# Mask products of the attention scores in 64x64 tiles of the matrix array in place of 64x128

## The chip, the cores and the metric

The kernel runs on one core of one Trainium2 chip. The metric is the device time of one execution in microseconds. Three executions of the kernel before took 1553.94, 1553.43 and 1547.58 us, with a median of 1553.43.

## The reference

Two layers run one after the other on 4096 tokens of 128 values (16 batches of 256 tokens). Each layer normalises the tokens, computes an attention `s` and a mixture of experts `g` from them, and adds `s * silu(g)` to the tokens. Cut to what matters here:

```python
# layer 0: differential attention, 16 heads of 8, two attention maps per head, causal
att1 = softmax(where(causal, q1 @ k1.T * scale, -inf))
att2 = softmax(where(causal, q2 @ k2.T * scale, -inf))
y = (att1 - lam * att2) @ v          # then normalised per head, and @ c_w
# layer 1: 16 heads of 8, each query sees a window of the last 128 keys
scores = q @ k_window.T / sqrt(8)    # keys before the start count as score 0
ctx = softmax(scores) @ v_window     # then @ wo.T + bo
```

In the first layer a query must not see later keys; in the second it must see neither later keys nor keys that lie 128 or more positions back. In both, -1e30 is added to a score that must not count, and that addition is what the change is about.

## The kernel before, in words

`build` (L1455) runs, for each layer, a layer norm, a router, the experts and the attention (`build_attention`, L709). The attention is laid out over five engines that run the same schedule (`schedule`, L873): a step for each batch, with a prologue, a loop of turns of four steps, and an epilogue. A step has `UNITS` slots (12 in the first layer, which has A = 2 attention maps, 6 in the second). In each slot TensorE makes two **groups** of score products, i = 0 and i = 1, one for each half of the heads (`both_scores`, L1118).

A group serves two streams at once. `scores_for_max` (L1071) makes scores with queries on the partitions, from which DVE takes row maxima (L1370). It runs ahead by `AHEAD` slots, so it works on the next batches. `scores` (L1093) makes scores with keys on the partitions, of the current batch, with the negated maxima folded in, and ACT takes their exponentials (L1259). The first stream reads the stack on partitions of half `i` and writes `s_bank[i]`; the second reads half `1 - i` and writes `t_bank[i]`. Each stream has two banks of 512 fp32 columns, so group i of a slot may begin when DVE and ACT have read what group i of the slot before wrote (`lone_wait` on `s_free` and `t_free`, L1126 and L1131).

For each j from 0 to 5 a product of the one stream and a product of the other are issued in turn, by `score_matmul` (L1057). j = 0 and j = 1 are the **mask products** (L1062): an identity times a table of mask values. A block of scores has 128 partitions and 128 or 256 columns. Only the two 64x64 blocks on its diagonal, or in windowed cases two more, have a mask that is neither all zero nor constant; whole blocks are masked by extra rows of the stack. The mask table (`R.mask_diag_q` and others, L1490 to L1493) has 64 rows, the same in both halves of the partitions, and the identity `R.eye` (L1489) is a 64x128 table in two forms: for j = 0 the identity stands in the left 64 columns and zeros in the right, for j = 1 the other way. So product j adds the mask to the 64 partitions of its block, and writes zeros to the other 64. The columns that it writes are those of block j (`one_block`, L1065: 64 columns of each of the 2 or 4 heads of the bank; `two_blocks`, L1068: 128 of each of 2 heads). The first has `start=True` and the second doesn't. The remaining 2 or 4 products (L1063) add a head's scores each, 256 or 128 columns, with `start=False`.

What widths meet in a slot follows from the code. In the second layer all mask products have 256 columns. In the first layer `scores_for_max` has 256 where n + 4 modulo 6 is 0 or 1 and 128 otherwise, and `scores` has 256 where n modulo 3 is 2 and 128 otherwise. Slots 0, 1, 4, 6, 7 and 10 have 128 columns in both streams; slots 2 and 8 with 256 in both; slots 3, 5, 9 and 11 with one of each.

Between groups TensorE does fp32 work. After both groups of a slot `weigh` (L1138) multiplies the exponentials with the values in 32-column tiles (L1153, then L1156, four strips that share a bank), and `general_use` (L1196) does one or two of: projections (L1044, L1051, L1188), transposes (L1164, L1172, L1179). DVE also splits the projected queries and keys into three bf16 pieces (`split`, the last part is L1358, in slot 2 of the first layer and slot 5 of the second). When they are ready, SP copies them with twelve DMAs into the stack (`fill_stack`, L999 to L1007). TensorE waits for these copies before the first maxima of that batch (`stacked`, L1125), in slot 8 of the first layer and slot 3 of the second.

Of the kernel before, what the change touches and what calls it, by code (L numbers as in the profile page):

```python
# [39 lines left out]
HALF = 64  # L40
# [665 lines left out]
def build_attention(nc, R, D, layer):  # L706
# [76 lines left out]
    with ExitStack() as ctx:  # L783
# [251 lines left out]
        def _(pe):  # L1035
# [21 lines left out]
            def score_matmul(j, bank, half, per, rows, fine, mask, left, right):  # L1057

                tile = slice(half * HALF, half * HALF + (HALF if j < 2 else rows))
                bank = bank.rearrange("p (m w) -> p m w", m=per)  # L1060
                if j < 2:
                    return nc.tensor.matmul(fine(bank, j), R.eye[tile, j, :], mask[tile], start=(j == 0), stop=True, skip_group_check=(j > 0))  # L1062
                return nc.tensor.matmul(bank[:, j - 2, :], left(j - 2)[tile], right(j - 2)[tile], start=False, stop=True, skip_group_check=True)  # L1063

            def one_block(at):  # L1065
# [481 lines left out]
```

## Time and profile before

| | |
|---|---|
| median of 3 executions | 1553.43 us |
| the profiled execution | 1545.69 us |
| its span, first to last instruction | 1544.0 us |
| TensorE matmul busy | 1163.1 us, 75% |
| DVE busy | 841.1 us, 54% |
| ACT busy | 782.4 us, 51% |
| GpSimd busy | 626.6 us, 41% |
| mean granted TensorE clock | 0.88 |
| mask products (L1062), matmuls | 2304, 235.8 us |
| score products (L1063), matmuls | 3072, 273.3 us |

The profiled execution is one of its own beside the three. Its rows name an engine, a line and a tile shape: 64*128 is a weight tile of 64 rows (contraction) and 128 columns (output partitions), and 64x256 beside it is the moving operand, 256 columns. Matmuls are pipelined and the end of one is modelled, so the busy time of TensorE is an upper bound, and the starts are what a reader should go by. PEld is TensorE's weight load. "x4" in a timeline is a merged run of four instructions; where two groups overlap, the start is that of the first of each. The first layer's attention runs from about 300 us to 860 us of the span, the second's from about 1150 us on.

### The profile page before, as it was taken

What the parts mean: (1) busy time and instruction counts of PE and PEld (TensorE: products, weight loads), DVE (VectorE), ACT (ScalarE), POOL (GpSimd) and SP (SyncE); (2) the same over time, 40 slices, a digit from 0 to 9 for tenths busy, and PEclk for the clock granted to TensorE, in tenths of its full rate; (3) what the DMA queues carried; (4) which work ended last, traced back from release to release, by engine and by line L of the source; (5) the groups of instructions that cost most, each with busy time, mean ns of one, the idle gap of its engine ahead of it and who ended that gap; (6) DMA issues with size and microseconds to landing.
All of it is one profiled execution on the core that took longest, in us unless ns stands there. A gap on an engine that the chain in (4) does not pass through costs nothing. (4 is left out here: it accounts for less than half of the span.)

```text
span 1544.0 us, 38917 instructions
## 1 busy us (share of the span) xinstructions
PE 1163.1 (75%) x12538; PEld 870.9 (56%) x12538; DVE 841.1 (54%) x1694; ACT 782.4 (51%) x1828; POOL 626.6 (41%) x968
## 2 busy tenths in 40 slices
PE   1458888768888788888888156888866788888885
PEld 1357888634555555555554146788853555555553
DVE  5184555456766676677641338455534655556551
ACT  2163544415777677777765130344441655555553
POOL 3254445200355445545554315444521234334434
PEclk9999999968999999999997555799985988878887
DMA  5401222231232223222300240122222112221210
GB/s 146 112 0 39 59 56 55 38 86 47 63 80 58 52 51 85 64 51 60 82 18 8 69 110 0 43 54 56 57 42 61 50 49 55 60 56 49 61 42 24
DMA packets 144971, 86.71 MB, mean 56 GB/s; under 512 B 16610, under 2 KB 138356, under 8 KB 144820
## 3 DMA queue, kind: packets, MB, share of 16 engines
q1 hardware_dynamic: 136116, 66.85, 16.6%
q0 software_dynamic: 8704, 17.84, 4.9%
q8 instruction: 95, 1.56, 0.4%
q14 instruction: 56, 0.46, 0.1%
HBM read 30.19 MB, written 15.73 MB: 30 GB/s over the span
## 5 line engine op out<-in xcount | busy, mean ns | idle before, releaser
L1370 DVE TENSOR_REDUCE at_maxima<-ps 128x2 f32<-128x512 f32 (+1 forms) x576 | 375.1, 685 | 270.8 <-PE ps L1063 250.0
L1259 ACT ACTIVATE at_probs<-ps 128x512 f32<-128x512 f32 x576 | 324.0, 597 | 133.2 <-PE ps L1063 115.8
L1062 PE MATMUL ps<-tables 64*128 64x256 bf16 (+1 forms) x2304 | 235.8, 266 | 154.0 <-DMA stack<-at_pieces 58.3
L1063 PE MATMUL ps<-stack 62*128 62x256 bf16 (+3 forms) x3072 | 273.3, 260 | 4.5 <-issue 4.5
L664 ACT ACTIVATE ex_hid<-ps,ex_w 128x128 f32<-128x128 f32 x576 | 163.8, 370 | 178.1 <-PE ps L639 130.8
L1062 PEld LDWEIGHTS ps<-tables 64*128 64x128 bf16 x2304 | 94.5, 97 | 263.9 <-issue 230.7
L598 POOL DMA_INDIRECT ex_rows<-xn_rows,ex_ids_now x144 | 149.8, 1041 | 93.8 <-PE ps L631 42.7
L1063 PEld LDWEIGHTS ps<-stack 62*128 62x128 bf16 (+1 forms) x3072 | 170.7, 101 | 16.3 <-issue 4.1
L639 PE MATMUL ps<-ex_rowsT,ex_w 128*128 128x128 f32 x1152 | 161.4, 284 | 24.1 <-DVE ex_rowsT L688 23.3
L695 DVE COPY ex_w<-weights 128x1156 f32 x144 | 114.0, 791 | 104.8 <-issue 103.8
L649 PE MATMUL ps<-ex_w,ex_hid 128*128 128x128 f32 x1152 | 154.8, 278 | 15.6 <-ACT ex_hid L664 7.2
L639 PEld LDWEIGHTS ps<-ex_rowsT,ex_w 128*128 128x128 f32 x1152 | 143.2, 195 | 33.2 <-issue 30.1
L649 PEld LDWEIGHTS ps<-ex_w,ex_hid 128*128 128x128 f32 x1152 | 141.8, 194 | 17.8 <-issue 17.7
L949 POOL DMA_INDIRECT at_chosen_y<-list_out,at_slot x128 | 126.6, 989 | 57.5 <-issue 33.1
L1153 PE MATMUL ps<-at_probs,at_v 128*32 128x256 f32 x1536 | 135.5, 427 | 3.3 <-ACT at_probs L1259 3.3
L970 POOL TENSOR_TENSOR at_s_rows<-at_s_rows,at_silu 128x256 f32<-128x256 f32 x32 | 23.3, 729 | 226.3 <-ACT at_s_rows L1311 226.3
L1156 PE MATMUL ps<-at_probs,at_v 128*32 128x128 f32 x1536 | 86.0, 295 | 1.6 <-issue 1.6
L1156 PEld LDWEIGHTS ps<-at_probs,at_v 128*32 128x32 f32 x1536 | 54.9, 120 | 42.9 <-issue 15.2
L424 PE MATMUL ps<-rt_at_tile,rt_at_place 128*128 128x72 f32 x256 | 55.2, 422 | 29.0 <-POOL rt_at_place L391 29.0
L1264 ACT COPY at_weighed_t<-ps 128x512 f32<-128x512 f32 x96 | 56.7, 591 | 39.2 <-remote 25.1
L894 POOL COPY at_xb<-xnT 128x256 f32<-128x256 f32 (+1 forms) x32 | 13.5, 421 | 155.1 <-PE ps L1054 96.6
L424 PEld LDWEIGHTS ps<-rt_at_tile,rt_at_place 128*128 128x128 f32 x256 | 54.8, 333 | 30.4 <-POOL rt_at_place L391 30.4
(181 smaller groups left out, 1610.4 us busy)
## 6 DMA issues: line engine op xcount, KB each, us to landing
stack<-at_pieces SPq DMA_DIRECT2D x192, 128.0 KB
stack<-at_pieces SPq DMA_DIRECT2D x192, 64.0 KB
list_out<-ex_result SPq DMA_DIRECT2D x144, 64.0 KB
weights<-in_L_w SPq DMA_DIRECT2D x4, 1024.0 KB, 6.1
weights<-in_L_w SPq DMA_DIRECT2D x16, 256.0 KB, 6.6
xn_rows<-xn SPq DMA_DIRECT2D x8, 512.0 KB, 3.2
ex_rows<-xn_rows,ex_ids_now POOLq DMA_INDIRECT x144, 2.5
x<-in_L_attn_x SPq DMA_DIRECT2D x4, 512.0 KB, 6.0
```

The costliest lines, as they stand in the source:

```text
L598: nc.gpsimd.indirect_dma_start(rows[q][:], None, D["xn_rows"], bass.IndirectOffsetOnAxis(ids[:, q:q + 1], 0)).then_inc(loaded[q], 16)
L639: last = nc.tensor.matmul(hid_ps[q % 2][:, hb * P:(hb + 1) * P], w[q][:, W1 + hb * P:W1 + (hb + 1) * P], rowsT[q % 2][:], start=True, stop ...
L649: last = nc.tensor.matmul(out_ps[q % 2][:, 0:C], hid[q % 2][:, hb, :], w[q][:, W2 + hb * C:W2 + (hb + 1) * C], start=(hb == 0), stop=(hb = ...
L664: last = nc.scalar.activation(hid[q % 2][:, hb, :], hid_ps[q % 2][:, hb * P:(hb + 1) * P], gelu, bias=w[q][:, B1 + hb:B1 + hb + 1])
L695: nc.vector.tensor_copy(w[q][:], weights[:, bass.ds(e, 1), :].rearrange("p o w -> p (o w)"))
L949: nc.gpsimd.indirect_dma_start(chosen_y[t][k][:], None, D["list_out"], bass.IndirectOffsetOnAxis(slot[:, i:i + 1], 0)).then_inc(gathered, 16)
L1062: return nc.tensor.matmul(fine(bank, j), R.eye[tile, j, :], mask[tile], start=(j == 0), stop=True, skip_group_check=(j > 0))
L1063: return nc.tensor.matmul(bank[:, j - 2, :], left(j - 2)[tile], right(j - 2)[tile], start=False, stop=True, skip_group_check=True)
L1153: nc.tensor.matmul(strip, v[p][:, 0, h, :], pr[:, part, at:at + SEQ], start=True, stop=False)
L1156: last = nc.tensor.matmul(strip[:, P:SEQ], v[p][:, 1, h, :], pr[:, 2, at:at + P], start=False, stop=True)
L1259: nc.scalar.activation(probs[:, (n // 3) % 2, n % 3, i * 512:(i + 1) * 512], t_bank[i], ACT.Exp, scale=SCALE).then_inc(t_free, 1)
L1370: nc.vector.tensor_reduce(by_half[:, h0:h0 + heads, a], s_bank[i].rearrange("p (m k) -> p m k", k=P * (late + 1)), AX.X, ALU.max).then_inc ...
```

## The change

Each mask product writes only the 64 partitions of its own block. The weight is the 64x64 identity, and the output begins at partition 0 for j = 0 and at partition 64 for j = 1. Both products have `start=True`. The score products are as they were; their first write to a region that no mask product wrote now fills it.

```diff
                 if j < 2:
-                    return nc.tensor.matmul(fine(bank, j), R.eye[tile, j, :], mask[tile], start=(j == 0), stop=True, skip_group_check=(j > 0))
+                    out = slice(j * HALF, (j + 1) * HALF)
+                    return nc.tensor.matmul(fine(bank[out], j), R.eye[tile, 0, 0:HALF], mask[tile], start=True, stop=True)
                 return nc.tensor.matmul(bank[:, j - 2, :], left(j - 2)[tile], right(j - 2)[tile], start=False, stop=True, skip_group_check=True)
```

## Rows read from the trace of the kernel before

**Rows 1.** Windows over the steady part of both attention stages: from:to, length, busy times

```profile
core 0: us, PE busy (x) PEld busy (x) DVE busy (x) ACT busy (x) POOL busy (x), PEclk, DMA share, GB/s
353.00:784.00 431.00, 363.23 (x5440) 235.38 (x5436) 297.82 (x485) 305.20 (x627) 198.87 (x337) 0.97 0.25 62
1190.00:1491.00 301.00, 249.50 (x2852) 162.97 (x2849) 170.88 (x342) 170.89 (x392) 112.99 (x185) 0.85 0.22 56
```

**Rows 2.** Waits: who waited for whom, us in total, times, longest

```profile
DVE at_maxima L1370 <- PE ps L1063: 250.0, 216, 11.1
PEld ps L1062 <- issue: 230.7, 396, 4.3
ACT at_probs L1259 <- PE ps L1063: 115.8, 181, 6.9
...
PE ps L1062 <- DMA stack<-at_pieces: 58.3, 26, 12.1
```

**Rows 3.** Groups by line and shape: count, busy us, mean ns, idle before

```profile
L1062 PE MATMUL ps<-tables 64*128 64x256 bf16 x1280 | 171.5, 298 | 120.2 <-DMA stack<-at_pieces 58.3 <-DVE at_maxima L1370 33.7 <-issue 15.2
...
L1062 PEld LDWEIGHTS ps<-tables 64*128 64x128 bf16 x2304 | 94.5, 97 | 263.9 <-issue 230.7 <-DMA stack<-at_pieces 23.0
```

**Rows 4.** Timeline of TensorE, first layer, 600 to 607 us: start, length, what

```profile
600.27 0.29 PE L1062 MATMUL ps<-tables 64*128 64x128 bf16 x4 [0.68 <-ACT at_probs L1259]
600.38 0.40 PE L1063 MATMUL ps<-stack 62*128 62x256 bf16 x4
600.77 0.29 PE L1062 MATMUL ps<-tables 64*128 64x128 bf16 x4
...
603.60 0.64 PE L1153 MATMUL ps<-at_probs,at_v 128*32 128x256 f32 x8
604.05 0.40 PE L1156 MATMUL ps<-at_probs,at_v 128*32 128x128 f32 x8
604.39 1.16 PE L1188 MATMUL ps<-wo,at_yT 128*128 128x128 f32 x8
605.48 0.39 PE L1062 MATMUL ps<-tables 64*128 64x256 bf16 x4
605.71 0.39 PE L1063 MATMUL ps<-stack 62*128 62x128 bf16 x8
605.93 0.38 PE L1062 MATMUL ps<-tables 64*128 64x256 bf16 x4
606.15 0.39 PE L1063 MATMUL ps<-stack 62*128 62x128 bf16 x8
606.47 0.66 PE L1164 MATMUL ps<-ident,at_weighed_t 128*128 128x128 f32 x4
607.12 0.38 PE L1062 MATMUL ps<-tables 64*128 64x256 bf16 x4
607.25 0.47 PE L1063 MATMUL ps<-stack 64*128 64x256 bf16 x6
```

**Rows 5.** Timeline of TensorE, second layer, 1293 to 1297 us

```profile
1292.96 0.61 PE L1062 MATMUL ps<-tables 64*128 64x256 bf16 x4
1293.36 0.64 PE L1063 MATMUL ps<-stack 62*128 62x256 bf16 x4
1293.79 0.64 PE L1062 MATMUL ps<-tables 64*128 64x256 bf16 x4
1294.22 0.64 PE L1063 MATMUL ps<-stack 64*128 64x256 bf16 x4
1294.78 1.08 PE L1153 MATMUL ps<-at_probs,at_v 128*32 128x256 f32 x8
...
1296.84 0.61 PE L1062 MATMUL ps<-tables 64*128 64x256 bf16 x4
```

**Rows 6.** Window over the same stretch; PEclk is the number after the POOL column

```profile
1290.00:1298.00 8.00, 8.00 (x55) 4.79 (x56) 3.79 (x7) 4.71 (x11) 0.40 (x1) 0.50 0.19 50
```

**Rows 7.** Timeline of SP's queue and of TensorE around one batch's stack copies

```profile
639.24 8.73 SPq L1007 DMA_DIRECT2D stack<-at_pieces  x12
...
651.11 0.39 PE L1062 MATMUL ps<-tables 64*128 64x256 bf16 x4 [1.44 <-DMA stack<-at_pieces]
```

## The prediction

> **What bounds the kernel now.** I read the windows first. In the two attention stages TensorE is busy for 84% and 83% of the time, DVE and ACT for 57 to 71%, at a mean granted clock of 0.97 and 0.85 [rows 1]. The list of waits says who is late: DVE idles 250.0 us and ACT 115.8 us for score products, TensorE idles 58.3 us in 26 places for the stack transfers [rows 2]. So TensorE leads, in a loop through DVE and ACT, and at one place a batch the transfers lead. 1280 of the 2304 mask products have 256 columns [rows 3], the other 1024 have 128.
>
> The timeline shows what they cost. The two row halves run at once, so four products are two pairs. From the first mask product of a group to its first score product it is 0.11 us with 128 columns (600.27 to 600.38), 0.23 with 256 (605.48 to 605.71), 0.13 where the halves differ (607.12 to 607.25) [rows 4]. That is streaming: a pair of 128 columns takes 0.055, since four score pairs last 0.22 (605.71 to 605.93). Nothing is lost between masks and scores; both use 64x128 tiles.
>
> **What a change of tile costs.** After the four pairs that start at 606.15 the 128x128 transposes start at 606.47: 0.32, of which 0.22 is streaming, so 0.10 is lost. A change of columns alone costs as much: L1156 (128x32) runs two rounds of four at 604.05, half as wide as L1153's, which last 0.45 together (603.60 to 604.05, the same tile and no gap); 0.34 later L1188 (128x128) starts, 0.11 more than the 0.23 that they stream [rows 4]. At a granted clock of 0.50, the level of 1.2 GHz, two score pairs that stream in 0.43 (1293.36 to 1293.79) are followed by L1153 after 0.56 (1294.22 to 1294.78): 0.13 lost [rows 5, 6]. The Trainium skill, TensorEngine Tiling (Array Packing), section Tiling Modes, says that a change of the tiling mode, not of the tile alone, drains TensorE. By that rule, and the trace agrees, this change pays a drain that the kernel now does without.
>
> **The change, part by part.**
> 1. It removes half of the mask streaming: the four products go to four tiles. L1153's four strips, four column tiles that write one bank, run together (eight products of 256 columns in 0.45), so I take the four as one round: 0.055 for 128 columns, 0.11 for 256, 0.20 at half clock.
> 2. It adds a switch from masks to scores in every group. No row has 64x64 to 64x128. Bounds: 0, if only the row split counted, and 0.13, the largest seen; I take 0.10, since the column-only row is nearest. Masks to scores is then 0.155 in place of 0.11 (+0.045), 0.21 in place of 0.23 (I count -0.01, for the four starts), 0.21 in place of 0.13 (+0.08), and at half clock 0.33 in place of 0.40 (-0.07).
> 3. It adds a switch from scores to the next masks where these follow directly. Between the two groups of a unit there often is a pause: 600.38 to 600.77 is 0.39 with 0.22 of streaming. A pause over 0.10 hides the drain and the first group's delay too; with that cover gone 0.10 more would show. There is none at 605.71 to 605.93 [rows 4]. The weight loads of masks sat idle for "issue" 396 times [rows 2] in 576 groups, which leaves 31% without: I take one unit in three in the first layer. In the second layer all products are 256 wide, the queue runs ahead (1293.36 to 1293.79 is streaming alone [rows 5]), and I take three in four; one in three and all are the bounds. Ahead of a unit's first group stands fp32 work, whose switch is paid already.
> 4. Weight loads of 64 columns replace loads of 128. A load's record has 97 ns [rows 3] and lies beside the product before it. Bounds: 0, hidden as now, and 0.05 a group, half of that record exposed; I take 0, since L1153's loads, in column tiles as well, cost nothing visible at 603.60 beyond the switch.
> 5. No wait, DMA, or instruction of DVE, ACT, SP or POOL is added, moved or removed.
>
> **What lies on the path.** A batch's stack copies start when L1358 is done: twelve issues from 639.24 on take 8.73 us, and TensorE takes its next mask at 651.11 after 1.44 idle [rows 7]. From slot 2 to slot 8 of the first layer that transfer sets the time, and there five units at about 0.09 each (0.44) vanish in the 1.44. In the second layer the copies start after the split in slot 5 and are needed in slot 3; a wait is 58.3 / 26 = 2.2 us on average [rows 2], again more than three units add. So 7 of 12 units count in the first layer (112 in 16 batches) and 3 of 6 in the second (48).
>
> First layer: the seven slots (8 to 11, 0 to 2) hold three groups of 128, two of 256, two mixed: (3 x 0.045 - 2 x 0.01 + 2 x 0.08) / 7 = +0.04 a group. A unit costs 0.04, and in one of three 0.14 more (the other group and the drain): 0.087 x 112 = 9.7 us. Second layer: at full clock -0.01 + 3/4 x (0.10 - 0.01) = +0.06, at half clock -0.07 + 3/4 x (0.13 - 0.07) = -0.025; a clock of 0.85 is 30% at half, so +0.034 x 48 = 1.7 us. Together 11.4. Not all is passed on, since a group also waits for DVE or ACT (0.68 at 600.27 [rows 4]) that were late with other work; I take 0.7, below TensorE's share of 0.84: **+8 us**. The profiled execution took 1545.69 us, 1.7 over its span of 1544.0; it becomes 1553.7. The median of the three runs, 1553.43, is 7.7 above that execution, and I carry the sum over to it: 1561.4.
>
> **Rivals.**
> - Faster: a column split inside one row split needs no drain. Place: masks to scores. A group then gains 0.055 (128), 0.115 (256), about 0.08 (mixed), 0.20 at half clock. First layer 4/3 x 0.08 x 112 = 12.0, second 1.75 x (0.7 x 0.115 + 0.3 x 0.20) x 48 = 11.8, times 0.7: -17, so 1537. It decides once a switch costs less than about 0.05. For it: no row shows exactly this pair of tiles. Against: the 0.11 of L1156 to L1188. Chance 0.15. (The page's section Overview, in the Trainium skill, promises up to twice the rate where the stationary operand has at most 64 columns, as here.)
> - Nothing to measure: pauses and the loop through DVE and ACT take up the 11 us as well. For it: most groups pause for longer than a switch. Against: DVE's 250.0 us of waiting. 1553, chance 0.20.
> - The four products don't overlap, so the change doesn't do what it says: the switches come on top of the old streaming. (0.10 + 1/3 x 0.20) x 112 = 18.7, second layer about 0.27 x 48 = 13, times 0.7: +22, 1575. L1153's strips speak against it. Chance 0.05.
> - The slower weight load of part 4: (0.067 x 112 + 0.0875 x 48) x 0.7 = 8 us more, 1569. For it: nothing covers a load right after a drain. Chance 0.05. The Trainium skill, TensorEngine Tiling (Array Packing), section Restrictions and Gotchas, says that column tiling excludes Fast Weight Load; its page TensorE: Matmul & The Clock Gate, section LDWEIGHTS, gives columns / 1.2 ns, an estimate of 53 ns for 64.
> - The clock: less is streamed, and the second layer runs at half clock for 60% in place of 30%. A unit at half clock lasts 1296.84 - 1292.96 = 3.88 [rows 5], at full clock about half of that: 0.3 x 48 x 1.94 x 0.7 = 20 on top, 1581. For it: the clock in that stage is unsteady (0.85). Against: TensorE's pauses don't grow. Chance 0.05.
>
> **How the numbers follow.** My own case has 0.50 and spans 1556 to 1573: from a third of the sum to its full (0.087 x 192 + 0.034 x 96) = 20 us, if no unit is covered. Half a per cent, about what a measurement of this kernel can tell from no change, is 7.8 us: 1545.7 to 1561.2. Rather more than half of my case lies above (0.30), which with the last three rivals makes 0.45 slower; 0.20 of it and the second rival make 0.40 the same; 0.15 faster. The range 1543 to 1577 leaves out most of the first rival and the last one.
>
> **What the profile of after would show.** Right: L1062 as 64x64, the four mask products of a group starting within 0.02; masks to scores about 0.16 with 128 columns and 0.21 with 256; scores to masks 0.10 over streaming where they follow directly; transfer waits somewhat shorter in total than 58.3. Wrong: masks to scores of 0.06 and 0.11 (the first rival), of 0.21 and 0.32 (no overlap), or a clock well under 0.85 in the second attention stage.

## The result, and the profile after

The kernel after takes 1588.35 us (median of 4, 1585.47 to 1591.51), the kernel before in the same comparison 1550.51 (median of 4). The ratio is 1.0245, with an interval of 1.0207 to 1.0284: 38 us slower, where +8 was forecast. The profiled execution took 1585.47 us and its span is 1583.5, against 1544.0. Every line from L1062 on has moved down by one, so L1063 are now the mask products and L1064 the score products.

The page of after: the row of TensorE, and its groups (busy us, mean ns, idle before).

```profile
PE 1235.1 (78%) x12538; PEld 836.1 (53%) x12538; DVE 842.8 (53%) x1694; ACT 793.2 (50%) x1828; POOL 630.0 (40%) x968
...
L1063 PE MATMUL ps<-tables 64*64 64x256 bf16 (+1 forms) x2304 | 194.5, 289 | 125.9 <-DMA stack<-at_pieces 52.6
L1064 PE MATMUL ps<-stack 64*128 64x128 bf16 (+3 forms) x3072 | 280.0, 269 | 0.0
...
L1063 PEld LDWEIGHTS ps<-tables 64*64 64x64 bf16 x2304 | 79.7, 107 | 269.6 <-issue 231.3
```

The change does what it says: the tile is 64*64, and the busy time of the mask products falls from 235.8 to 194.5 us. The transfer wait is somewhat shorter, 52.6 in place of 58.3 [rows 2], as forecast. A weight load's record grows from 97 to 107 ns [rows 3].

The list of waits of after, to be held against [rows 2]:

```profile
DVE at_maxima L1371 <- PE ps L1064: 271.0, 227, 11.1
...
PEld ps L1063 <- issue: 231.3, 484, 3.8
ACT at_probs L1260 <- PE ps L1064: 130.6, 213, 5.6
...
PE ps L1063 <- DMA stack<-at_pieces: 52.6, 20, 12.1
```

DVE and ACT wait longer for TensorE, by 21 and 15 us. The idle time of a mask's weight load keeps its sum, but it comes 484 times in place of 396, in 626 groups (526 with four mask products, 100 with two): many groups that followed the scores directly now stand behind a short gap.

The timeline of TensorE of after, first layer, answers to [rows 4]:

```profile
619.01 0.30 PE L1063 MATMUL ps<-tables 64*64 64x256 bf16 x4
619.24 0.40 PE L1064 MATMUL ps<-stack 62*128 62x128 bf16 x8
619.57 0.66 PE L1165 MATMUL ps<-ident,at_weighed_t 128*128 128x128 f32 x4
620.15 0.30 PE L1063 MATMUL ps<-tables 64*64 64x256 bf16 x4
620.39 0.39 PE L1064 MATMUL ps<-stack 62*128 62x128 bf16 x6
620.71 0.30 PE L1063 MATMUL ps<-tables 64*64 64x256 bf16 x4
...
622.91 0.25 PE L1063 MATMUL ps<-tables 64*64 64x128 bf16 x4 [0.20 <-issue]
623.09 0.39 PE L1064 MATMUL ps<-stack 62*128 62x256 bf16 x4
```

From the first mask product to the first score product it is 0.18 with 128 columns (622.91 to 623.09; it was 0.11), 0.23 with 256 (619.01 to 619.24, as before), and 0.24 where the halves differ (620.15 to 620.39; it was 0.13). Scores to masks, 620.39 to 620.71, takes 0.32, of which some 0.22 is streaming: 0.10 lost, where [rows 4] lose nothing.

Windows show where the 38 us lie. They are read from the two profiled executions, whose spans differ by 39.5 us. Each kernel is cut at its first mask product of a layer and at the first exponentials (L1260) of batch 0, of batch 15, and the last. The rows are, in order: layer 0 up to the first exponentials, its steady part, its last batch, the same three of layer 1, and the end. The number behind the POOL column is the mean granted clock. First before, then after:

```profile
319.40:353.40 34.00, 27.04 (x174) 15.71 (x174) 23.98 (x38) 3.39 (x8) 4.35 (x6) 0.60 0.22 56
353.40:812.10 458.70, 386.73 (x5789) 250.52 (x5790) 312.30 (x511) 325.68 (x670) 212.99 (x362) 0.97 0.24 59
812.10:839.60 27.50, 25.86 (x263) 14.59 (x261) 2.12 (x6) 18.28 (x39) 14.05 (x25) 0.71 0.04 11
1163.40:1190.10 26.70, 20.09 (x114) 11.95 (x116) 15.89 (x30) 2.80 (x8) 0.53 (x2) 0.56 0.14 36
1190.10:1506.40 316.30, 264.51 (x3018) 172.60 (x3015) 178.21 (x358) 181.69 (x418) 119.35 (x197) 0.85 0.21 54
1506.40:1520.20 13.80, 12.33 (x134) 7.31 (x132) 1.48 (x5) 9.18 (x21) 6.75 (x13) 0.88 0.09 25
1520.20:1544.00 23.80, 9.69 (x60) 5.78 (x60) 2.29 (x6) 4.39 (x12) 8.20 (x13) 0.66 0.08 22
```

```profile
320.70:357.70 37.00, 34.84 (x178) 15.30 (x178) 25.12 (x38) 3.36 (x7) 4.35 (x6) 0.50 0.20 51
357.70:833.10 475.40, 423.31 (x5788) 235.34 (x5784) 312.50 (x510) 331.27 (x671) 213.96 (x362) 0.93 0.23 57
833.10:865.40 32.30, 31.54 (x264) 15.86 (x264) 3.11 (x6) 19.37 (x38) 14.04 (x25) 0.66 0.04 9
1191.20:1219.00 27.80, 23.11 (x114) 9.94 (x114) 16.47 (x30) 2.83 (x9) 0.53 (x2) 0.50 0.13 34
1219.00:1537.60 318.60, 273.29 (x3037) 150.10 (x3034) 177.71 (x358) 185.15 (x418) 122.94 (x198) 0.85 0.21 55
1537.60:1558.50 20.90, 18.86 (x114) 8.87 (x114) 1.45 (x5) 9.75 (x21) 7.79 (x13) 0.50 0.07 20
1558.50:1583.50 25.00, 11.99 (x60) 7.42 (x60) 1.90 (x6) 4.37 (x12) 5.41 (x10) 0.50 0.04 10
```

Three findings. The steady part of layer 0 grows by 16.7 us, and its clock falls from 0.97 to 0.93. The steady part of layer 1 grows by 2.3, at an unchanged 0.85. And the five short stretches around them, which the prediction never looked at, grow by 3.0, 4.8, 1.1, 7.1 and 1.2: 17.2 us together, in 126 us. The first four (16.0 us) are the **one-stream steps**: a group serves one stream only (maxima ahead of batch 0, scores of batch 15) and has two mask products in place of four. In four of the five TensorE is now at 0.50, the level of 1.2 GHz, from end to end. The last batch of layer 1 goes from 13.8 us at 0.88 to 20.9 at 0.50.

### The profile page after: what moved, and what is told of

Same layout as the page of the kernel before. It is cut to its first block and busy times, and to the rows that moved or that the text cites. A ratio compares the mean times of both kernels' runs of the same rounds, so it can differ in the third digit from the quotient of the medians.

```text
span 1583.5 us, 38917 instructions
## 1 busy us (share of the span) xinstructions
PE 1235.1 (78%) x12538; PEld 836.1 (53%) x12538; DVE 842.8 (53%) x1694; ACT 793.2 (50%) x1828; POOL 630.0 (40%) x968
## 5 line engine op out<-in xcount | busy, mean ns | idle before, releaser
L1260 ACT ACTIVATE at_probs<-ps 128x512 f32<-128x512 f32 x576 | 330.0, 598 | 142.6 <-PE ps L1064 130.6
L1063 PE MATMUL ps<-tables 64*64 64x256 bf16 (+1 forms) x2304 | 194.5, 289 | 125.9 <-DMA stack<-at_pieces 52.6
L1064 PE MATMUL ps<-stack 64*128 64x128 bf16 (+3 forms) x3072 | 280.0, 269 | 0.0
L1063 PEld LDWEIGHTS ps<-tables 64*64 64x64 bf16 x2304 | 79.7, 107 | 269.6 <-issue 231.3
L598 POOL DMA_INDIRECT ex_rows<-xn_rows,ex_ids_now x144 | 148.8, 1034 | 96.5 <-PE ps L631 50.1
L1064 PEld LDWEIGHTS ps<-stack 64*128 64x128 bf16 (+1 forms) x3072 | 116.0, 98 | 77.1 <-issue 24.0
L949 POOL DMA_INDIRECT at_chosen_y<-list_out,at_slot x128 | 127.4, 995 | 57.1 <-issue 32.7
L1154 PE MATMUL ps<-at_probs,at_v 128*32 128x256 f32 x1536 | 141.1, 444 | 3.4 <-ACT at_probs L1260 3.4
L1265 ACT COPY at_weighed_t<-ps 128x512 f32<-128x512 f32 x96 | 56.7, 591 | 38.2 <-PE ps L1157 25.5
L1044 PE MATMUL ps<-xnT,wqk 128*128 128x256 f32 (+1 forms) x192 | 65.0, 456 | 9.8 <-POOL at_v L978 9.2
```

The costliest lines, as they stand in the source:

```text
L598: nc.gpsimd.indirect_dma_start(rows[q][:], None, D["xn_rows"], bass.IndirectOffsetOnAxis(ids[:, q:q + 1], 0)).then_inc(loaded[q], 16)
L949: nc.gpsimd.indirect_dma_start(chosen_y[t][k][:], None, D["list_out"], bass.IndirectOffsetOnAxis(slot[:, i:i + 1], 0)).then_inc(gathered, 16)
L1063: return nc.tensor.matmul(fine(bank[out], j), R.eye[tile, 0, 0:HALF], mask[tile], start=True, stop=True)
L1154: nc.tensor.matmul(strip, v[p][:, 0, h, :], pr[:, part, at:at + SEQ], start=True, stop=False)
L1260: nc.scalar.activation(probs[:, (n // 3) % 2, n % 3, i * 512:(i + 1) * 512], t_bank[i], ACT.Exp, scale=SCALE).then_inc(t_free, 1)
```

## The experiments

Eighteen kernels. The table gives, for each, the ratio to the kernel before with its interval, and length / mean granted clock of the windows cut as above: layer 0's first step (A), steady part (B), last batch (C); layer 1's first step (D), steady part (E), last batch (F).

Each row of windows comes from one profiled execution, and that is not always a middling one. Those of `e_edge` (1591.90 us, median 1584.56), `e_doubled_edge` (1601.69, median 1592.82) and `e_not89` (1587.92, median 1581.64) were the slowest of their four, that of `e_steady` (1565.05, median 1570.59) the fastest. E shows how far one trace can be trusted. In the seven kernels with before's order, products and waits in all of it (before, `e_layer0`, `e_only89`, `e_doubled_89` and the shifts) it lies between 316.0 and 320.0. With the change in layer 1's steady part it was 318.6 in after and 317.1 in `e_steady`, but 326.0 in `e_layer1` and in `e_not89`.

| kernel | ratio | A | B | C | D | E | F |
|---|---|---|---|---|---|---|---|
| before | 1 | 34.0 / .60 | 458.7 / .97 | 27.5 / .71 | 26.7 / .56 | 316.3 / .85 | 13.8 / .88 |
| after | 1.0245 [1.0207, 1.0284] | 37.0 / .50 | 475.4 / .93 | 32.3 / .66 | 27.8 / .50 | 318.6 / .85 | 20.9 / .50 |
| e_layer0 | 1.0164 [1.0125, 1.0204] | 37.0 / .50 | 478.0 / .92 | 32.3 / .66 | 26.7 / .50 | 317.9 / .85 | 13.0 / 1.00 |
| e_layer1 | 1.0070 [1.0042, 1.0099] | 34.1 / .60 | 458.3 / .97 | 25.0 / .91 | 27.8 / .50 | 326.0 / .85 | 21.0 / .50 |
| e_half | 0.9827 [0.9793, 0.9860] | 32.7 / .60 | 450.1 / .93 | 25.9 / .72 | 25.4 / .50 | 312.3 / .83 | 13.8 / .88 |
| e_doubled | 1.0710 [1.0665, 1.0756] | 40.4 / .50 | 516.5 / .92 | 29.7 / .86 | 29.8 / .50 | 345.3 / .85 | 24.0 / .50 |
| e_all64 | 1.0376 [1.0310, 1.0441] | 34.8 / .60 | 503.0 / .88 | 25.8 / .73 | 25.7 / .50 | 325.0 / .82 | 17.5 / .80 |
| e_grouped64 | 1.0282 [1.0212, 1.0353] | 38.8 / .59 | 487.2 / .92 | 27.6 / .72 | 27.1 / .50 | 319.3 / .84 | 12.0 / 1.00 |
| e_grouped128 | 1.0221 [1.0150, 1.0291] | 38.4 / .59 | 481.3 / .95 | 26.6 / .84 | 27.7 / .50 | 322.1 / .85 | 12.0 / 1.00 |
| e_fill_before | 1.0332 [1.0297, 1.0367] | 34.6 / .60 | 463.1 / .96 | 24.9 / .91 | 25.1 / .64 | 371.9 / .85 | 20.1 / .66 |
| e_fill_after | 1.0586 [1.0553, 1.0619] | 37.9 / .55 | 477.8 / .95 | 32.4 / .66 | 26.9 / .63 | 387.0 / .82 | 19.5 / .57 |
| e_steady | 1.0161 [1.0111, 1.0210] | 33.5 / .60 | 478.8 / .92 | 27.3 / .71 | 26.7 / .50 | 317.1 / .85 | 13.8 / .88 |
| e_edge | 1.0197 [1.0146, 1.0248] | 36.9 / .50 | 472.4 / .94 | 38.5 / .50 | 27.9 / .50 | 324.2 / .85 | 21.0 / .50 |
| e_doubled_edge | 1.0245 [1.0205, 1.0286] | 40.2 / .50 | 466.3 / .95 | 42.3 / .50 | 29.6 / .50 | 328.0 / .84 | 22.9 / .50 |
| e_not89 | 1.0205 [1.0151, 1.0260] | 36.6 / .50 | 472.7 / .95 | 31.9 / .66 | 27.8 / .50 | 326.0 / .83 | 19.6 / .57 |
| e_only89 | 1.0068 [1.0031, 1.0105] | 33.5 / .60 | 470.8 / .91 | 24.8 / .91 | 26.7 / .50 | 318.1 / .85 | 12.9 / 1.00 |
| e_doubled_89 | 1.0214 [1.0175, 1.0252] | 35.0 / .60 | 494.9 / .92 | 28.0 / .72 | 26.8 / .50 | 317.4 / .87 | 13.7 / 1.00 |
| e_shift2 | 1.0004 [0.9978, 1.0030] | 34.6 / .60 | 459.7 / .96 | 26.7 / .73 | 26.8 / .50 | 320.0 / .85 | 12.8 / 1.00 |
| e_shift4 | 0.9985 [0.9955, 1.0015] | 34.5 / .60 | 456.7 / .97 | 24.7 / .91 | 26.8 / .50 | 316.0 / .87 | 12.8 / 1.00 |
| e_shift7 | 1.0014 [0.9981, 1.0047] | 35.6 / .64 | 459.2 / .96 | 27.7 / .71 | 27.3 / .50 | 317.6 / .84 | 12.8 / 1.00 |

### The change in one layer

```diff
+                if j < 2 and layer == 0:
+                    out = slice(j * HALF, (j + 1) * HALF)
+                    return nc.tensor.matmul(fine(bank[out], j), R.eye[tile, 0, 0:HALF], mask[tile], start=True, stop=True)
                 if j < 2:
...
```

`e_layer1` has `layer == 1` there.

> The change in the first layer's attention alone. Two theories. S (switches): the two drains in each group of score products are paid on the path, and the lower clock is a by-product. C (clock): the change streams less, the granted clock falls more often, and that costs most of the 38 us. Both read the two traces alike here: of the 39.5 us between the profiled executions some 27 us fall into the first layer's attention, so the ratio to the kernel before should be about 1.017 (+27 us). S expects about +20 to +27 with the clock of that stage anywhere, C expects the time to follow the us at half clock in that stage.

> The change in the second layer's attention alone: the rest, about +12 us, of which the traces show only 2 between the first exponential of batch 0 and that of batch 15, and 7 in the last batch, where the changed kernel ran wholly at half clock. S expects +3 to +8 (the last batch's 7 us would be chance), C expects +8 to +14 with the last batch at half clock again.

The medians were 1580.69 and 1567.09 us. The ratios add up to the whole (0.0164 + 0.0070 = 0.0234 against 0.0245). Layer 1 alone takes 12.0 us more than before by the medians (1555.08 for before here), with the last batch wholly at half clock again: the forecast of theory C, so those 7 us are not chance. In its trace F is longer by 7.2 us and E by 9.7, where after's E was longer by 2.3 with the same products. Where layer 0 is unchanged, B is that of before.

### Less streaming without a switch, and the switch without less streaming

`e_half` leaves out the mask products of j = 1 in both layers, so half of the blocks are not masked; the tiles are those of before. `e_doubled` has the 64x64 tiles and issues each mask product twice.

```diff
-                for j in range(6):
+                for j in (0, 2, 3, 4, 5):
```

```diff
+                    for _ in range(2):
+                        last = nc.tensor.matmul(fine(bank[out], j), R.eye[tile, 0, 0:HALF], mask[tile], start=True, stop=True)
+                    return last
```

> The kernel before with the mask products j = 1 left out (half of the masks are missing from the scores), so the mask streaming is halved as in the change, but in 64x128 tiles with no switch. S expects a kernel faster than before: 0.055 to 0.11 us less a group, -10 to -25 us, clock near 0.88. C expects the clock to fall to about 0.85 as in the change and the time to stay at or above that of before.

> The changed kernel with each 64x64 mask product issued twice, so that as much is streamed as before and all the switches stay. S expects it to be slower than the change by the streaming that comes back, +10 to +25 us on 1588, so 1598 to 1613. C expects the clock to come back to about 0.88 and the time to fall below the change's, 1565 to 1585.

The medians were 1530.26 and 1665.17 us. Timeline of TensorE, `e_half`:

```profile
600.58 0.28 PE L1062 MATMUL ps<-tables 64*128 64x256 bf16 x2
600.70 0.39 PE L1063 MATMUL ps<-stack 62*128 62x128 bf16 x8
```

Masks to scores is 0.12 in place of 0.23 (0.06 with 128 columns, as a median over the groups). Halving the mask work is worth 1.7% when it brings no switch: the saving that the change was after exists, and the change loses it. The time is that of theory S (25 us less than before), but the clock is nearer to C: 0.86 over the whole kernel, and B is at 0.93 as in after. So in layer 0's steady part fewer mask columns go with a lower clock although no tile changes, and B is 8.6 us shorter even so. Its window F is at 0.88 like before's, though it streams as little as after; `e_doubled`, which streams as much as before, has F at 0.50. So in the one-stream steps it isn't the missing columns that lower the clock. By the ratios `e_doubled` is 72 us slower than after, far more than either theory allowed; its extra products and weight loads cost time of their own in B and E, so it is no pure measure of the switch.

### No change of tile between masks and scores

`e_all64` splits each score product into two of 64x64, so that the tile doesn't change inside a unit.

```diff
+                for c in range(2):
+                    out = slice(c * HALF, (c + 1) * HALF)
+                    last = nc.tensor.matmul(bank[out, j - 2, :], left(j - 2)[tile, out], right(j - 2)[tile], start=False, stop=True, skip_group_check=True)
```

> The change with the score products in 64x64 tiles as well: each is issued as two of 64 output partitions, so nothing switches between masks and scores, and the mask streaming stays halved. S expects the 38 us to be gone and the gain of halved masks without switches to show, as in e_half, 1525 to 1550, if issuing twice as many score products and loads is not the new limit; each adds at least the 0.007 us that four column tiles start apart. If the extra issue binds, 1560 to 1600. C expects no gain over the change.

Measured 1598.95 us. Timeline of TensorE:

```profile
603.17 0.25 PE L1063 MATMUL ps<-tables 64*64 64x128 bf16 x4 [0.37 <-DVE at_maxima L1374]
603.23 0.41 PE L1066 MATMUL ps<-stack 62*64 62x256 bf16 x8
```

Masks to scores is 0.06, against 0.18 in after: the 0.12 is the price of the change from 64x64 to 64x128, since the mask products are the same in both. (The Trainium skill, TensorEngine Tiling (Array Packing), section Tiling Modes, has a change of the tiling mode drain TensorE; these two rows agree.) Yet the kernel is slower than after, though there are no drains inside a group: 1.0376 against 1.0245. That more products have to be started and loaded isn't what the trace shows as the reason. B is 27.6 us longer than in after, and 28 us of that lie in two slots, 7 (from 3.40 to 4.25 us on average) and 9 (from 3.06 to 4.08, half clock in 14 of 15 batches); what lengthens them is not shown. It also shows that a window F with few drains keeps most of its clock (17.5 at 0.80).

### Both groups' masks first, then both groups' scores

One change between 64x64 and 64x128 in a slot in place of three. The second kernel has the same order with the tiles of before, and so no such change:

```diff
-                for j in range(6):
+                for js in ((0, 1), (2, 3, 4, 5)):
+                    for i in range(2):
+                        for j in js:
...
-                    for i in range(2):
-                        both_scores(step, r, n, i)
+                    both_scores(step, r, n)
```

> The changed kernel with the order inside a slot altered: the mask products of both groups first, then the score products of both, so that a slot has one switch between 64x64 and 64x128 where the change has three. If the 38 us are switches on the path (S), this gives most of them back: two switches of 0.09 us in 288 slots, partly hidden today, -12 to -30 us against the change, 1558 to 1576. If they come from the clock alone (C), the streaming is that of the change and the time stays at 1580 to 1592.

> The control of the run beside it: the same order in the kernel before (64x128 tiles, no switch). It tells what the order does by itself: the second group's masks now stand ahead of the first group's scores, so DVE and ACT get the first bank 0.11 to 0.22 us later in a slot, but the second group has no wait of its own. 1545 to 1575; e_grouped64 should lie above it by one switch a slot less half of the mask streaming, 0 to +15 us.

Medians 1583.44 and 1575.63 us, beside 1542.4 for before. With before's tiles this order alone costs 2.2%, since the first group now waits for the reader of the second one's bank: TensorE's wait for DVE goes from 45.1 to 137.0 us. On top of that the 64x64 tiles cost 6 us in B, a third of what they cost in after, and nothing in F, which stays at 1.00: in this order, with one such change a slot, the step keeps its clock. `e_grouped64` did not come back to the 1558 to 1576 us of theory S, since the order eats what the switches give back.

### A filler against the fall of the clock

Products of 512 columns ahead of the transfer wait, 5 in layer 0 and 10 in layer 1, with the tiles of before and of after:

```diff
+                        if has(step, "shift"):
+                            bank = general(step, "shift")
+                            for _ in range(5 if layer == 0 else 10):
+                                nc.tensor.matmul(bank, R.tables[:, 0:P], R.tables[:, 256:768], start=True, stop=True)
```

> The same useless work in the kernel before. Its clock rarely falls in slots 8 and 9 of the first layer, but often in the second layer (92 us of 316 at half). C: 0 to -12 us against before, all of it from the second layer. S: 0 to +10.

> The changed kernel with useless work in a wait: before TensorE waits for a batch's stack copies it issues bf16 products of 512 columns in 128x128 tiles into the bank that the next transpose will overwrite, 5 (1.1 us) in the first layer and 10 (2.1 us) in the second. The clock fell to half in slots 8 and 9 of the first layer in 10 and 11 of 15 batches of the changed kernel, against 3 and 4 before. C, in the form that the clock falls because TensorE streams too little around that wait: the clock of the steady first layer returns to before's (some 29 us at half in place of 69) and slots 8 and 9 lose about 0.5 us a batch, so -8 to -16 us against the change, 1572 to 1580. S (the switches' own time): the filler is at best hidden, 1586 to 1600.

Medians 1606.6 and 1647.07 us. It misses: E is longer by 56 us with the tiles of before and by 68 with those of after. In the trace of `e_fill_before` the fillers of E (L1128) are themselves 30.6 us long, so they aren't hidden in the wait, and TensorE idles 12.8 us before them, 9.8 of it for ACT to read the bank; where the rest comes from was not traced. In layer 0, B with filler is 463.1 and 477.8, so the tiles still cost 15 us although the clocks (0.96 and 0.95) are nearly the same.

### The steady part alone, the one-stream steps alone

The 64x64 form stands under `if j < 2 and narrow[0]`, and `both_scores` sets it. In `e_steady` and in `e_edge`:

```diff
+                narrow[0] = bool(ahead) and now
```

```diff
+                narrow[0] = bool(ahead) != bool(now)
```

> The change only where a group serves both streams; in the first and last steps of each layer, where a group serves one stream, the mask products are those of before. The stage table puts about 18 of the 39.5 us into those steps (3.1 + 4.8 + 1.1 + 1.1 + 7.1 + 1.3), all of them at half clock nearly throughout. If that is caused there, this kernel takes 18 us less than the change: 1570, and its last batch 14 us in place of 21. If the last batch's 7 us come from what the steady part leaves behind, or from chance, 1580 to 1590.

> The change only where a group serves one stream (the first step of each layer's attention, which has maxima alone, and the last, which has scores of the last batch alone); two 64x64 mask products there, everything else as before. The kernel with the change everywhere else took 24 us more than before, and its one-stream steps were as before. Theory A (the one-stream steps are worth some 18 us by themselves): first mask to first exponential 37 in layer 0 and 28 in layer 1, last batch 32 and 21, all or nearly all at a granted clock of 0.50; the rest as before; 1566 to 1570 us, ratio about 1.011. Theory B (they are slow only because TensorE comes into them out of a steady part that the change has slowed): little remains, 1552 to 1556, ratio 1.000 to 1.003.

`e_doubled_edge` is `e_edge` with each of its 64x64 products issued twice:

> As the run with the change in the one-stream steps alone, but each 64x64 mask product there is issued twice, so that as many columns stream as before. Theory A (changes of tile): the last batch of layer 1 stays at 21 to 24 us, wholly at a granted clock of 0.50, the other one-stream steps at 27 to 40 as with single products, 1566 to 1574 us, ratio about 1.012 to 1.015. Theory B (less streaming lowers the clock): the clock is as before in these steps, last batch of layer 1 at 14 to 16, the four steps together within 6 us of the kernel before, 1552 to 1558 us, ratio about 1.003.

The medians were 1570.59, 1584.56 and 1592.82 us. Windows A, B, C and F of `e_edge`:

```profile
320.20:357.10 36.90, 34.77 (x176) 15.33 (x178) 25.11 (x38) 3.36 (x7) 4.34 (x6) 0.50 0.20 51
357.10:829.50 472.40, 396.78 (x5788) 255.26 (x5788) 312.34 (x510) 325.84 (x670) 212.09 (x362) 0.94 0.23 58
829.50:868.00 38.50, 37.81 (x264) 17.75 (x264) 2.73 (x6) 19.86 (x39) 13.98 (x25) 0.50 0.03 8
...
1545.60:1566.60 21.00, 18.85 (x114) 8.84 (x114) 1.45 (x5) 9.77 (x21) 7.76 (x13) 0.50 0.07 20
```

Windows C and F of `e_doubled_edge`:

```profile
827.10:869.40 42.30, 40.96 (x310) 18.95 (x308) 2.71 (x6) 19.62 (x39) 13.99 (x25) 0.50 0.03 8
...
1552.20:1575.10 22.90, 22.56 (x151) 10.10 (x150) 1.41 (x5) 9.81 (x21) 7.77 (x13) 0.50 0.07 19
```

`e_steady` has every one-stream window of before within half a microsecond. It is 18 us faster than after by the medians and 13 by the ratios (1.0161 against 1.0245), which compare each with the kernel before in the same round. `e_edge` has them slow and wholly at half clock. With the streaming restored they stay so. The one-stream steps are therefore slow through the changes of tile that they themselves hold: theory A in both. But `e_edge` came out at 1584.56, not at 1566 to 1570, and the excess is a surprise. In its trace, which is 7 us slower than its median, B is 472.4 in place of 458.7, although from batch 0 to batch 14 TensorE's mask products there are those of before, save in the last four slots of one step, where no maxima are left to run ahead. E is 7.9 longer as well. By the medians `e_edge` is 34 us slower than before, 22 of which are the four one-stream windows; so some 11 us fall elsewhere.

### Slots 8 and 9

In B of after, the starts of ACT's exponentials show one slot that grows far more than the rest: slot 9, from 2.46 to 3.06 us on average, 9 us over 15 batches. Slots 8 and 9 are at half clock for a part of their time in more batches (slot 8 in 10 of 15 in place of 3, slot 9 in 11 in place of 4). They come right behind the transfer wait. The other slots with a direct change of tile (0, 1, 2, 10 and 11) grow at full clock by 0.37 us a batch in all. The two slots were left out of the change, and then changed alone:

```diff
+                narrow[0] = not (layer == 0 and n in (8, 9))
```

```diff
+                narrow[0] = layer == 0 and n in (8, 9)
```

The first is `e_not89`, the second `e_only89`.

> The change everywhere but in slots 8 and 9 of the first layer, where the clock fell more often and slot 9 took 0.60 us more a batch. Theory L: the clock falls because of what these slots stream and drain themselves: slot 9 goes back to 2.5 us, 9 us less than the change, 1579. Theory H: it falls because of the halved masks in the slots before the transfer wait: slot 9 stays near 3.0, 1586 to 1590.

> The complement: the change in slots 8 and 9 of the first layer alone. Theory L: +8 to +12 us against before (slot 9 at 3.0). Theory H: the switches' own time alone, 0 to +4 us.

The medians were 1581.64 and 1558.22 us, beside 1546.37 for before: `e_only89` as theory L had it, `e_not89` between the two. The two slots alone bring 12 us in B and slot 9 to 3.18 us; all others without them bring 14, and slot 9 to 2.78. The parts of B don't add up: 12 + 14 is more than the 17 of the whole. `e_doubled_89` has the two slots with each 64x64 product issued twice:

> The kernel before, with the mask products of slots 8 and 9 of the first layer in 64x64 tiles, each of them issued twice (two of the same product one behind the other, so that the tables add the same mask, and about as many columns are streamed as with the 64x128 tiles). It stands beside the run with the single 64x64 products in the same two slots, 1558.2 us, 1.0068, whose stage between the first and the last exponentials of layer 0 was 470.7 us with 81.6 at a granted clock of 0.50, slot 9 lasting 3.18. Theory A (the clock falls in these slots because less is streamed before and after the transfer wait): with the streaming back the clock is as in the kernel before; slot 9 about 2.6, that stage about 462 us with some 30 at half clock, 1550 to 1554 us, ratio about 1.001. Theory B (it falls because the changes of tile leave TensorE idle): slot 9 at 3.2 or more, that stage 470 to 476 with 80 or more at half clock, 1558 to 1564 us, ratio 1.007 to 1.012.

It took 1585.92 us: B is 494.9 at 0.92, slot 9 lasts 3.96 us. More streaming does not bring the clock back, so theory A falls, but B is 19 us above what theory B allowed. Slots 7, 8 and 9 hold nearly all that it has over before (0.53, 0.24 and 1.50 us a batch). The lists of waits over 353 to 850 us have one kind of row that grew there. `e_doubled_89`, then before:

```profile
ACT at_probs L1267 <- remote: 19.6, 9, 3.1
...
DVE at_maxima L1378 <- remote: 12.6, 4, 3.6
```

```profile
ACT at_probs L1259 <- remote: 3.0, 4, 1.2
...
DVE at_maxima L1370 <- remote: 1.1, 1, 1.1
```

"remote" is idle time that ended with the count of a semaphore before which the view finds no instruction that had just ended. A batch of `e_edge` shows it; the timeline of TensorE, DVE and ACT in slot 8, with the tiles of before:

```profile
664.30 0.40 PE L1068 MATMUL ps<-stack 64*128 64x128 bf16 x8
...
665.40 0.47 PE L1068 MATMUL ps<-stack 64*128 64x256 bf16 x6
...
667.41 0.69 DVE L1376 TENSOR_REDUCE at_maxima<-ps 128x4 f32<-128x512 f32 x1 [2.44 <-remote]
667.44 0.60 ACT L1265 ACTIVATE at_probs<-ps 128x512 f32<-128x512 f32 x1 [2.36 <-remote]
...
668.40 0.38 PE L1067 MATMUL ps<-tables 64*128 64x256 bf16 x4 [2.53 <-DVE at_maxima L1376]
```

The same place in the kernel before:

```profile
651.77 0.40 PE L1063 MATMUL ps<-stack 64*128 64x128 bf16 x8
...
652.87 0.47 PE L1063 MATMUL ps<-stack 64*128 64x256 bf16 x6
...
653.93 0.69 DVE L1370 TENSOR_REDUCE at_maxima<-ps 128x4 f32<-128x512 f32 x1 [1.49 <-PE ps L1063]
653.96 0.60 ACT L1259 ACTIVATE at_probs<-ps 128x512 f32<-128x512 f32 x1 [1.58 <-PE ps L1063]
...
654.92 0.38 PE L1062 MATMUL ps<-tables 64*128 64x256 bf16 x4 [1.58 <-issue]
```

Both readers take the group whose score products start at 664.30 (651.77 in before) and end, as modelled, at 664.70 (652.17). They begin together, 2.7 us after that end in `e_edge` and 1.8 in before. TensorE needs the banks that they read for the group after next, and is idle meanwhile.

Who is late can be read from the trace, which also has the time at which each semaphore is counted up. TensorE's two counts for this group come at 667.39 and 667.42 in `e_edge`, at 653.90 and 653.94 in before, and each reader begins 0.02 us after its count. So DVE and ACT are not late. TensorE's count is, and the modelled ends of its rows hide that. The counts of the next group, modelled to end at 665.87, follow at 667.56 and 667.60.

This stall of TensorE is in every kernel of the table, and in the kernels compared here it is not longer with changed tiles. Of ACT's 359 groups with a recorded count in B, 37 have it more than 0.3 us after the modelled end in before, and 35 of 359 in after, all in slots 8 to 11. Merged, these late stretches come to 53.0 us in before, 48.6 in after, 47.6 in `e_edge` and 54.3 in `e_doubled_89`. The sums on "remote", 32 us in `e_doubled_89` and 4 in before, are therefore no measure of the stall.

In all 20 traces every count of TensorE that comes more than 0.5 us after the last product that can have made it (251 of 2053 in before, 261 of 2045 in after) lies within 1.5 us of a record of one of GpSimd's indirect DMAs (L949 here, L598 in the experts), and only a third of all its counts lie so near to one. In before, after and `e_edge` no count of DVE or ACT is that late. No run moved these DMAs, so that they cause the stall is not shown.

### Is it only how the batches fall in time?

Since `e_edge` lost 14 us in a part that it does not change, three kernels shift the first layer's start and change no mask product (2, 4 and 7 extra projection products in the step before batch 0):

```diff
+                if layer == 0 and isinstance(step, int) and step == -1 and i == 0:
+                    for _ in range(2):
+                        nc.tensor.matmul(bank[:, 0:SEQ], R.wqk[layer][:, 0, :], R.xnT[:, bass.ds(b * SEQ, SEQ)], start=True, stop=True)
```

> The kernel before with one delay: in the last step before batch 0 of the first layer TensorE issues one fp32 projection product of 256 columns two times more than it needs (some 0.9 us at full clock, twice that at half), and nothing else is changed. The run with 64x64 masks in the one-stream steps alone took 34 us more than before, 14 of them in the steady part of layer 0, whose instructions were those of before, with half clock in slots 8 and 9 of most batches. Theory A (in the steady part the low stretches hit or miss the batches' transfer wait by how the two fall in time, and any shift of the start changes how many hit): the steady part of layer 0 leaves 458.8 us with 28.7 at half clock by more than the few us between equal runs; with this delay or with one of the two longer ones it is at 465 or more with 45 or more at half clock, and the three differ among themselves. Theory B (the tile changes lower the clock, in some way that lasts): the steady part stays at 457 to 461 with 25 to 35 at half clock in all three, and the time is that of before plus the delay, here 1552 to 1555, ratio about 1.001.

> As the run with two more products, with four (some 1.8 us at full clock, 3.6 at half). Theory A: a number at half clock of its own, anywhere from 28 to 80 us in the steady part of layer 0, and 1550 to 1575 us. Theory B: steady part as before, 1553 to 1556 us, ratio about 1.002.

> As the run with two more products, with seven (some 3.2 us at full clock, 6.3 at half). Theory A: a number at half clock of its own, anywhere from 28 to 80 us in the steady part of layer 0, and 1552 to 1578 us. Theory B: steady part as before, 1554 to 1559 us, ratio about 1.004.

The medians were 1547.98, 1546.41 and 1547.9 us, beside 1546.42 for before. B is 459.7, 456.7 and 459.2: within 2 us of before in each. Theory A falls, as far as these shifts reach: A grew by only 0.6, 0.5 and 1.6 us, and after's A grew by 3.0. But `e_steady` and `e_only89` have no longer A (33.5), and their B is longer by 20 and 12 us. The steady part of the kernel before is robust against a shift, and B is longer by 12 to 20 us in each of the six kernels that differ from it by single 64x64 mask products somewhere in layer 0 (after, `e_layer0`, `e_steady`, `e_edge`, `e_not89`, `e_only89`), by 7.6 in `e_doubled_edge`, and by at most 1 us in the four with before's products in that part (`e_layer1` and the shifts).

## Why the prediction was wrong

The direction was right and the time was 11 us above the upper end of the range. Step by step:

- **Streaming, part 1: right.** The four mask products run as one round; masks to scores in the kernel without switches is 0.06 with 128 columns, as taken.
- **The switch from masks to scores, part 2: right, slightly undersized.** It was put at 0.10; after and `e_all64` differ by 0.12. Masks to scores came out at 0.18 for 0.155 and at 0.23 and 0.24 for 0.21, and at half clock at 0.36 for 0.33 (median of 45 groups of the second layer).
- **The switch from scores to masks, part 3: right.** 0.10 at full clock.
- **Weight loads, part 4:** the record is 10 ns longer; no run measured them by themselves.
- **The cover by the transfer: right.** From the end of the split to the first maxima of the batch that waits it was 12.39 us and is 12.47, on average over batches 3 to 14; in the other half of the loop these batches got longer by 1.3 us each. TensorE's wait for the transfer in B went from 16.5 us in 14 places to 12.3 in 9. The average wait of 2.2 us was too high for the steady parts, where it is 1.2 in the first layer (16.5 / 14) and 1.8 in the second (16.4 / 9): 25.5 of the 58.3 us lie ahead of the two batches 0.
- **Slots 8 to 11 and 0 to 2:** the direct cost of 0.37 a batch at full clock in slots 0, 1, 2, 10 and 11 is 0.07 a unit, near the 0.087. Layer 1's steady part came to +2.3 for 1.7 in the trace of after, but to +9.7 in that of `e_layer1`. Together 0.37 x 16 + 2.3 = 8.2, near the forecast +8. That is luck in part: the +8 is 0.7 of a sum in which slots 8 and 9 are counted, the 8.2 leaves them out and takes the lower of two values for layer 1.
- **What lies on the path: failed, by omission.** The step counts "7 of 12 units count in the first layer (112 in 16 batches) and 3 of 6 in the second", as if all steps were the steady one. Its "576 groups" are the same slip: 2304 / 4, where the kernel has 626, of which 100 have two mask products. In the one-stream steps only half as many products stand between two changes of tile and nothing else fills TensorE. They cost 16.0 us, where the sum had nothing beyond a steady step's share, and the end of the kernel behind them 1.2. The runs show it both ways, by `e_steady` and by `e_edge`.
- **The clock: failed.** It stood as a rival with 0.05, placed in the second layer's steady part, where it did not move (0.85 in both), and it was dismissed with "TensorE's pauses don't grow". They do grow in number: 88 more weight loads of masks stand behind a gap (484 for 396), with the same sum. It fell in the one-stream steps, to 0.50, and in layer 0's slots 8 and 9, to half in two batches of three. The prediction had rows of the kernel at 0.85 and 0.97 on average and never asked where the clock was close to falling.

What stays open is a good part of the 16.7 us in B. Some 9 of them lie in slot 9, which is at half clock more often. It is shown that changed products in slots 8 and 9 are enough for a longer slot 9 (`e_only89`, 3.18 us) and that they are not needed for it (`e_edge`, 3.17). A shift of the start by up to 1.6 us doesn't do it, and restored streaming doesn't undo it (`e_doubled_89`). The stall beside the indirect DMAs is as long in before. The time at half clock alone doesn't explain it either: with the filler B differs by 15 us at nearly the same clock, and `e_half` has B at 0.93 and slot 9 at 2.49 us, as in before. Why changed tiles at another place bring slot 9 to half clock, no run tells.

## What to carry to other kernels

Count changes of TensorE's tile before counting the columns that a smaller tile saves: here a switch costs 0.10 to 0.12 us, as much as 256 columns at full clock, and `e_half` shows that the saved columns alone would have been worth 1.7%. Cost a change in the prologue and the epilogue as well as in the steady part: there the groups are thinner, nothing covers a gap, and with a few more gaps the clock was at 0.50 for the whole step. And don't read slots as independent: a part of the kernel whose instructions are unchanged can lose time as well (by the medians some 11 of the 34 us of `e_edge`). Last, the end of a matmul in a timeline is modelled: when a reader seems late, look for the time at which TensorE's semaphore was counted.

## What the runs showed of the hardware

- Four 64x64 products with 128 columns run together: with no change of tile behind them (`e_all64`) the next product follows 0.06 after the first, about the 0.055 in which one of them streams.
- A change of tile from 64x64 to 64x128 on the same rows costs 0.12 us, so the column split alone makes the difference.
- Two 64x64 products in place of one 64x128 for all scores, with no drain inside a group, made a slower kernel than after, which has the drains (ratios 1.0376 and 1.0245). The loss is in two slots of layer 0 and not in every group.
- The last batch of layer 1 runs in 12.0 to 13.8 us at a granted clock of 0.88 to 1.00, with before's order of products and tiles, and also where two groups share a change of tile. It takes 19.6 to 24.0 at 0.50 to 0.57 in each kernel that changes the tile in every one of its groups, with halved and with restored streaming. One trace breaks the pattern: `e_fill_before` takes 20.1 at 0.66 in this batch, with before's tiles and no filler in it. So changed tiles are one way to lose the clock there, and not the only one.
- The semaphore count that tells of a finished product of TensorE can come up to 3.8 us after the product's modelled end (B of before), and DVE and ACT start 0.02 after the count. In all 20 traces each count of TensorE over 0.5 us late (251 of 2053 in before) lies within 1.5 us of an indirect DMA of GpSimd.
